# Sharing out the attention loop of a shifted-window block anew: three small VectorE jobs to ScalarE, one to GpSimd, and a new order

## What is computed

```
xn   = layernorm(x) * g1 + b1
xw   = windows(roll(xn, -3, -3))                       # 1024 windows of N=49 tokens
q,k,v = split(xw @ qkv_w + qkv_b)                      # 6 heads of 8
attn = softmax(q * 8**-0.5 @ k.T + rpb + MASK)
out  = (attn @ v) @ proj_w + proj_b
x1   = x + roll(unwindow(out), 3, 3)
h    = layernorm(x1) * g2 + b2
y    = x1 + gelu(h @ fc1_w + fc1_b) @ fc2_w + fc2_b
```

## Time and profile before

| | |
|---|---|
| three runs | 1214.75, 1219.42, 1219.89 us |
| profiled execution | 1203.71 us, its span 1201.9 us |
| busy share of the span | PE 82%, PE weight load 66%, DVE 88%, ACT 77%, POOL 68% |
| mean granted TensorE clock | 0.955 of full speed |
| DMA | 64.50 MB, mean 54 GB/s |
| instructions | 47188 |

### The profile page before, as it was taken

One profiled execution on the slowest core, in us unless ns is written; L12 is line 12 of the kernel. 1 busy time (PEld: TensorE's weight loads), 2 busy tenths in 40 slices (PEclk: granted clock), 3 DMA queues, 4 the chain that ended last, 5 costly groups with the idle time before them and its releaser, 6 DMA issues. The chain is left out here.

```text
span 1201.9 us, 47188 instructions
## 1 busy us (share of the span) xinstructions
PE 990.5 (82%) x16452; PEld 798.1 (66%) x16452; DVE 1055.9 (88%) x2454; ACT 928.1 (77%) x2242; POOL 812.9 (68%) x907
## 2 busy tenths in 40 slices
PE   1588888989888898888888988898882888878877
PEld 0377777777777777777777777777771555555555
DVE  6799899989999999999999999999964888999996
ACT  0378787777877777777787778788773889999997
POOL 6267676666766666666666666677654767888883
PEclk9999999999999999999999999999995889999999
DMA  1122222222222222222222222222210011111111
GB/s 49 38 63 74 63 56 63 67 64 56 60 66 62 61 57 67 65 61 55 60 70 63 56 60 71 64 60 72 54 43 0 29 32 35 35 35 40 35 35 48
DMA packets 87016, 64.50 MB, mean 54 GB/s; under 512 B 53699, under 2 KB 86756, under 8 KB 86966
## 3 DMA queue, kind: packets, MB, share of 16 engines
q1 hardware_dynamic: 86966, 63.83, 20.1%
HBM read 10.48 MB, written 9.63 MB: 17 GB/s over the span
## 5 line engine op out<-in xcount | busy, mean ns | idle before, releaser
L376 POOL TENSOR_TENSOR pl<-p,ph 113x294 f16<-113x294 f32 x512 | 393.2, 777 | 163.8 <-ACT p L435 159.2
L221 POOL TENSOR_TENSOR rstd<-var,mhalf 112x7 f32<-112x7 f32 x128 | 192.6, 1505 | 134.3 <-DVE var L216 134.3
L741 DVE TENSOR_REDUCE rowmax<-banks 113x12 f32<-113x588 f32 x256 | 192.3, 751 | 55.4 <-PE banks L564 52.9
L433 ACT ACTIVATE ph<-banks 113x294 f16<-113x294 f32 x512 | 216.1, 422 | 25.4 <-PE banks L580 21.6
L580 PE MATMUL banks<-Qh,KAg 128*128 128x147 f16 x2048 | 223.7, 232 | 0.0
L435 ACT ACTIVATE p<-banks 113x294 f32<-113x294 f32 x512 | 213.9, 418 | 0.0
L580 PEld LDWEIGHTS banks<-Qh,KAg 128*128 128x128 f16 x2048 | 171.8, 99 | 34.1
L596 PE MATMUL banks<-Vb,ph 113*128 113x36 f16 x3072 | 184.0, 181 | 1.1 <-POOL pl L376 1.1
L596 PE MATMUL banks<-Vb,pl 113*128 113x36 f16 x1536 | 169.4, 180 | 0.0
L596 PEld LDWEIGHTS banks<-Vb,ph 113*128 113x128 f16 x3072 | 161.4, 97 | 11.0 <-POOL pl L376 1.4
L408 ACT ACTIVATE KM<-banks,lorow 128x392 f16<-128x392 f32 x128 | 75.2, 587 | 103.7 <-PE banks L498 103.6
(11 more groups left out here) (120 smaller groups left out, 2891.1 us busy)
## 6 DMA issues: line engine op xcount, KB each, us to landing
Qh<-QAB SPq DMA_DIRECT2D x192, 98.0 KB, 2.2
Vb<-Vn SPq DMA_DIRECT2D x256, 54.0 KB, 2.0
xres<-in_x SPq DMA_DIRECT2D x64, 147.0 KB, 2.2
KAh<-KA SPq DMA_DIRECT2D x192, 49.0 KB, 1.9
out_y<-ybuf SPq DMA_DIRECT2D x64, 147.0 KB, 2.0
Qh<-mT SPq DMA_DIRECT2D x128, 4.6 KB, 2.2
w<-in_weights SPq DMA_DIRECT2D x1, 278.9 KB
mask<-in_maskt SPq DMA_DIRECT2D x1, 257.2 KB
```

Source lines behind the costliest of these rows:

```text
L221: nc.gpsimd.tensor_tensor(rstd[:, :], var[:, :], mhalf[:, :], ALU.pow).then_inc(s_pow, 1)
L376: nc.gpsimd.tensor_tensor(pl[p % 4][:, :, :, 0:N].rearrange("p a w n -> p w a n"), p32[p % 4][:, :, :, :], ph[p % 4][:, :, :, 0:N].rearran ...
L433: nc.scalar.activation(ph[p % 4][:, :, :, 0:N].rearrange("p a w n -> p w a n"), src, ACT.Exp, scale=1.0 / SB)
L741: nc.vector.tensor_reduce(rowmax[:, 2 * p:2 * p + 4, :].rearrange("p (k w) a -> p k (w a)", k=2), sc[0:AP_, :, 0:2 * COLS].rearrange("p k ...
```

## The change

Every instruction of the attention phase is still there, and each computes the same values; four have gone to another engine, and most of the order is new. The MLP phase is not touched.

- `nmean` (the mean of 7 numbers per partition, negated) and `var` go from DVE to ACT, as copies with a scale (and a bias). `var` stands behind the first two exponentials of a step on ACT, `nmean` in the middle of it. Two semaphores that were kept by DVE's order (`s_pow`, `s_xc`) are now waited for by ACT.
- `KAg` of head group 0 goes from DVE to ACT (a copy with the mask column as scale). Group 1 stays on DVE, and moves from the middle of the step to its end. The semaphore `s_kg` becomes two.
- The low part of the output (`otok`, before on DVE line 826) goes to POOL, at the end of its step. DVE's `normalize` of half 0 waits for it.
- PE's transpose of `m16` moves from the end of a step to the start of the next; piece 0 of the plain scores of unit t+1 moves from the start of step t+1 to the end of step t; the `pv`, `t_scores`, `out` and `v` pieces change places.
- On ACT the square moves from the start of a step to the end of the one before, exponential 4 from the end of a step to the start of the next. On POOL the low parts of pieces 3 to 5 move into the next step.

```
+        def ln_mean_scalar(act, n):
+            wait(act, s_xc, n - 1)
+            act.wait_ge(s_sum, n)
+            nc.scalar.activation(nmean[:, :], ssum[:, :], ACT.Copy, scale=-1.0 / C).then_inc(s_mean, 1)
+        def ln_variance_scalar(act, n):
+            act.wait_ge(s_pow, n)
+            act.wait_ge(s_sqsum, n)
+            nc.scalar.activation(var[:, :], sqsum[:, :], ACT.Copy, bias=EPS, scale=1.0 / C).then_inc(s_var, 1)
...
 # GpSimd
+                    low(t - 2, 3)
+                    low(t - 2, 4)
                     ln_rsqrt(pool, t + 3)
+                    low(t - 2, 5)
                     ln_scale(pool, par, t + 3)
...
+                    pool.wait_ge(s_ohi, done(t - 2))
+                    nc.gpsimd.tensor_tensor(otok[:, :, C:2 * C], on[:, :, :], otok[:, :, 0:C],
+                                            ALU.subtract).then_inc(s_olo, 1)
...
 # ScalarE
-                    ln_square(act, par, t + 3)
+                    exp(t - 2, 4)
                     exp(t - 2, 5)
+                    ln_variance_scalar(act, t + 3)
                     k_high(0)
...
                     exp(t - 2, 7)
+                    wait(act, s_st, PAIRS * done(t - 2))
+                    act.wait_ge(s_klow, 2 * done(t))
+                    nc.scalar.activation(KAg[par][:, :, 0, 0:N], KA[par][:, :, :], ACT.Copy,
+                                         scale=grow[:, 0:1]).then_inc(s_kg[0], 1)
                     q_high(0)
+                    ln_mean_scalar(act, t + 4)
...
                     v_high()
-                    exp(t - 1, 4)
+                    ln_square(act, new, t + 4)
...
 # TensorE
+                    pe.wait_ge(s_m16, done(t - 1))
+                        pe.wait_ge(s_vlow, done(t))
+                    nc.tensor.transpose(psT[:, 0:AP_], m16[:, :], idt[0:AP_, 0:AP_]).then_inc(s_mtp, 1)
                     k_piece(0)
-                    scores(t, par, 0)
                     scores(t, par, 1)
-                    pv(t - 2, par, 3)
...
                     t_scores(t - 1, new, 4)
+                    scores(t + 1, new, 0)
                     t_scores(t - 1, new, 5)
+                    pv(t - 1, new, 1)
                     pv(t - 1, new, 2)
-                    pe.wait_ge(s_m16, done(t))
-                        pe.wait_ge(s_vlow, done(t + 1))
-                    nc.tensor.transpose(psT[:, 0:AP_], m16[:, :], idt[0:AP_, 0:AP_]).then_inc(s_mtp, 1)
...
 # VectorE
-                    ln_variance(dve, t + 3)
-                    for g in range(G):
-                        i = block(KAg[par], KA[par][:, :, :], g)
-                    i.then_inc(s_kg, 1)
-                    wait(dve, s_xc, t + 3)
-                    ln_mean(dve, t + 4)
+                    wait(dve, s_olo, done(t - 3))
                     normalize(0)
...
                     v_low()
-                    dve.wait_ge(s_ohi, done(t - 2))
-                    nc.vector.tensor_tensor(otok[:, :, C:2 * C], on[:, :, :], otok[:, :, 0:C],
-                                            ALU.subtract).then_inc(s_olo, 1)
+                    wait(dve, s_st, PAIRS * done(t - 2))
+                    dve.wait_ge(s_klow, 2 * done(t))
+                    block(KAg[par], KA[par][:, :, :], 1).then_inc(s_kg[1], 1)
```

More of the change, by code:

```diff
@@ L156, in swin_block_kernel @@
         s_qg = sem("q_blocks_ready")
-        s_kg = sem("k_blocks_ready")
+        s_kg = [sem(f"k_blocks_of_group{g}_ready") for g in range(G)]
         s_vz = sem("v_blocks_cleared")
@@ L391, in step @@
                 if exists(t - 1):
-                    for p in range(2, 6):
-                        low(t - 1, p)
+                    low(t - 1, 1)
+                    low(t - 1, 2)
+                if exists(t - 2):
+                    pool.wait_ge(s_ohi, done(t - 2))
+                    nc.gpsimd.tensor_tensor(otok[:, :, C:2 * C], on[:, :, :], otok[:, :, 0:C],
+                                            ALU.subtract).then_inc(s_olo, 1)
             def tables():
@@ L459, in step @@
                     ln_high(act, t + 3)
+                if exists(t - 1):
+                    exp(t - 1, 1)
                 if exists(t + 1):
@@ L475, in step @@
                     nc.scalar.activation(otok[:, :, 0:C], on[:, :, :], ACT.Copy).then_inc(s_ohi, 1)
[L476 to L477 removed]
+                if exists(t + 1):
+                    v_high()
+                if exists(t + 3):
+                    ln_square(act, new, t + 4)
             def tables():
@@ L572, in t_scores @@
                         pe.wait_ge(s_tb[upar], blocks_of(u, upar))
-                        pe.wait_ge(s_kg, done(u))
+                        for g in range(G):
+                            pe.wait_ge(s_kg[g], done(u))
                         pe.wait_ge(s_mrow, 16 * G * done(u))
@@ L598, in pv @@
                     i.then_inc(s_pv, 1)
+                if exists(t - 1):
+                    pe.wait_ge(s_m16, done(t - 1))
+                    if exists(t):
+                        pe.wait_ge(s_vlow, done(t))
+                    else:
+                        wait(pe, s_OT, done(t - 4))
+                    nc.tensor.transpose(psT[:, 0:AP_], m16[:, :], idt[0:AP_, 0:AP_]).then_inc(s_mtp, 1)
                 if exists(t + 1):
@@ L635, in step @@
                     pv(t - 2, par, 5)
+                if exists(t):
+                    scores(t, par, 6)
                 if exists(t + 1):
@@ L661, in step @@
                     t_scores(t - 1, new, 4)
+                if exists(t + 1):
+                    scores(t + 1, new, 0)
+                if exists(t - 1):
                     t_scores(t - 1, new, 5)
+                    pv(t - 1, new, 1)
                     pv(t - 1, new, 2)
-                if exists(t):
-                    pe.wait_ge(s_m16, done(t))
-                    if exists(t + 1):
-                        pe.wait_ge(s_vlow, done(t + 1))
-                    else:
-                        wait(pe, s_OT, done(t - 3))
-                    nc.tensor.transpose(psT[:, 0:AP_], m16[:, :], idt[0:AP_, 0:AP_]).then_inc(s_mtp, 1)
             def tables():
@@ L711, in k_low @@
                     if j == 0:
-                        wait(dve, s_kg, done(t - 1))
+                        for g in range(G):
+                            wait(dve, s_kg[g], done(t - 1))
                         wait(dve, s_sb, 16 * HP * done(t - 1))
@@ L779, in step @@
                     ln_sum(dve, t + 3, t + 4)
-                if exists(t - 2):
-                    normalize(0)
                 if exists(t + 1):
                     k_low(1)
+                if exists(t - 2):
+                    invert_sums(0)
                 if exists(t):
                     rmax(4)
-                    wait(dve, s_st, PAIRS * done(t - 2))
-                    dve.wait_ge(s_klow, 2 * done(t))
-                    for g in range(G):
-                        i = block(KAg[par], KA[par][:, :, :], g)
-                    i.then_inc(s_kg, 1)
+                if exists(t - 2):
+                    wait(dve, s_olo, done(t - 3))
+                    normalize(0)
                 if exists(t + 1):
```

32 lines of the change are left out of this document (12 added, 20 removed).

## The result

| | before | changed |
|---|---|---|
| median of the runs | 1217.36 us (1214.75 to 1219.89, 4 runs) | 1130.62 us (1129.78 to 1136.63, 4 runs) |
| ratio, 95% interval | 1 | 0.930 (0.926 to 0.934) |
| profiled execution, its span | 1203.71, 1201.9 us | 1130.22, 1128.4 us |

The account below looks back on a forecast made before the run. DVE was taken to bound the attention phase, with PE next; about 60 steps falling from 13.36 to 12.0 us take 82 us from 1203.7, giving 1122, taken as 1125 us, range 1092 to 1180 us.

Parts of the forecast that it names:

- DVE bounds, PE waits for its tail: Attention step: DVE's 12.3 us plus 0.9 us wait fill it; PE stands 1.2 us before the `m16` transpose, for `v_low`.
- The sum of four jobs, 1.7 us off DVE: `nmean` 0.54, `otok` 0.54, `KAg` 0.58, `var` hardly anything: DVE's need per step falls from 12.3 to 10.6 us.
- What it adds elsewhere: Per step, ACT's need rises from 10.4 to 11.4 us (`KAg`, `var`, `nmean`), POOL's from 9.0 to 10.0 (`otok`).
- PE's need: PE's matmuls in an attention step stay the same, 11.3 us, making PE the next bound.
- The walk's new waits: In one new step, PE loses 0.4 us for low K and 0.25 for `QAg`; DVE loses 0.4 for `xtok`.
- The branch: Loop end on PE: 0.1 of the 0.37 us delay was to stay, 0.05 us a step.
- The clock: PE's lower clock after the double gap costs 1.0 us of that step; granted clock was to be 1.00 throughout.
- The offset of 11 to 16 us between runs and profiled execution: Runs of before lie above their profile; if lower-clock steps cause it, it goes, else the median comes near 1135 us.
- the sum of 1122: Whole kernel: 60 steps x (13.36 - 12.0) = 82 us off the profiled 1203.7 us.
- B: New waits on ACT take more of the gain: step 12.5 to 13.0 us, 1152 to 1182 us; chance 0.15.
- C: Lower clock stays with PE as bound, 1.2 us in every second step: 1172 us; chance 0.08.
- D: ACT becomes the bound through `sqsum`, `var`, `KM`, K half: slower, step 13.7 us, 1237 us; chance 0.05.

Follow-up runs that it names:

- duties_kag_late: Kernel before, old order, `nmean` and `KAg` moved to ACT, low `otok` to POOL, variance left on DVE, `KAg` at the end of ACT's step: step 12.34 us, ratio 0.952.
- order_only: Changed kernel with its new order but all four jobs back on DVE: step 12.77 us, ratio 0.973 to the kernel before.
- duties_only: Kernel before with its old order, the four jobs moved to ACT and POOL: step 13.69 us, ratio 1.014.
- var_km_scores0: Changed kernel with ACT's variance behind the first `KM` and plain scores 0 behind transposed scores 5 on PE: step 11.52 us, 1105.08 us, ratio 0.912.

## Why the prediction was right, and where it was not

The time was to be 1125 us, in a range of 1092 to 1180; measured were 1131. The step was to be 12.0 us and is 12.02. The mechanism came as forecast, but the closeness of both numbers is in part luck, as the points show:

- *DVE bounds, PE waits for its tail.* The first half is shown, in either order: with the new order and the jobs back on DVE, DVE is busy 383 of 400 us, and in the old order, once `KAg` on ACT is out of the way, three jobs less on DVE bring the step at full clock from 13.09 to 12.34 us (duties_kag_late). PE's wait before the transpose was a sign of it rather than a cost of its own: order_only has it before `QAg` in place of the transpose, and duties_kag_late keeps 0.92 us of it.
- *The sum of four jobs, 1.7 us off DVE.* Too high: DVE's busy time fell from 12.3 to 11.0 us and not to 10.6. `KAg` and `otok` together measured 0.96 us a step against the 1.12 that I had taken (0.35 and 0.61 against 0.58 and 0.54). `nmean`, taken at 0.54, is the term that failed: its duration in the rows was a wait for POOL, and such a wait does not leave DVE with the instruction. With `nmean` on ACT the low part of `xtok` takes 773 ns in place of 504, beside a `pl`. That DVE has 0.4 us more to do than forecast did not show in the step, as PE bounds.
- *What it adds elsewhere.* `KAg` on ACT took 967 ns (0.94 expected) and in duties_only 0.86 us of ACT's list (0.82 expected, with an overlap that no row gave), `var` 208 and `nmean` 216 (about 0.15), the subtraction on POOL 930 (0.97). The bound of 0.6 for a tiny ACT instruction was far too wide.
- *PE's need.* PE is busy 11.6 us a step where 11.3 were expected, and idle 0.46 where waits and branch were to make 0.7. The two errors cancel, and that is why 12.0 fits so well.
- *The walk's new waits.* All three came: low part of K 0.26 (0.4), `xtok` 0.32 (0.4), `QAg` 0.39 (0.25). Taking the first and the last away one after the other gave 0.25 and 0.30 us a step, so both were on the path.
- *The branch.* Wrong. I left 0.1 us of it in a pair of steps, since PE's sequencer could run ahead; 0.33 us is still there.
- *The clock.* Right in kind: no even step with a lower clock is left. It had no term of its own; it is a quarter of the gain (0.34 of 1.37 us).
- *The offset of 11 to 16 us between runs and profiled execution.* The four runs of the changed kernel stand 0.4 us below to 6.4 above their profiled one. That the offset was due to steps at the lower clock, as the forecast of 1125 took it, is not shown. Some 7 us or more of it may lie in the MLP phase, which was shorter in the profile of before than in any other. The attention phase gained 79 us and not 82, and the MLP phase of the changed kernel's profile was 6.9 us longer: these two make up the distance between the sum of 1122 and the profiled execution of 1130.
- *Rivals.* B and C did not come. D, ACT becoming the bound through the K halves, is not what the changed kernel does, but what the same jobs do in the old order is near it: duties_only is slower than before. I had argued it down by the transpose's wait moving away, and that comes only with the order. Its path was another than mine, over `xtok` and not over the variance.

The Trainium skill's rule that moving work between VectorE and GpSimd might not help (page Perfetto Trace Analysis, section Optimizing Scalar/DVE Operations) did not decide here: undoing the move costs 0.61 us. Its ground, the port shared under a lock, fits the rows that surprised me: `nmean` 157 ns or 700 beside `pl`, `QAg` 428, 559, 667 or 882 on average, centring 748 or, started beside `xtok`, 1014.

Not settled: why the branch costs PE 0.33 us in the changed kernel while long and short steps are nearly alike in order_only (12.81 and 12.72), where DVE bounds, and in var_km_scores0 (11.53 and 11.51), where PE is busy 99%; and how much of the gain comes from each single move of the order, which was only tried as a whole. Nor was duties_kag_late tried with `otok` or `KAg` alone, so that its 1.10 us has no shares.

## What to carry to other kernels

Before giving work to a less busy engine, follow the rings of waits once round that the new engine's list is part of (here transpose, K half, `KM`, `xtok`, `v_low`), also those that have slack now: once the first bound is relieved, the next ring bounds, and work put into its stretch on the new engine is paid there. The same four moves were worth -0.25 us a step in the old order and +0.70 in the new one; in the old order, three of them with `KAg` 17 instructions further down were worth +1.10. So try the cheap change of place first, before a new order. A tiny VectorE instruction with a long duration may be waiting for GpSimd: see what runs beside it, and ask whether its neighbour will wait in its place once it has moved.

## What the hardware showed that I had not expected

- A loop body of four or of ten steps made PE stop at the branch for up to 4.8 us. With a body of two a long step differs from a short one by 0.33 us in the changed kernel, by 0.46 in the one before, and by 0.1 or less in order_only and var_km_scores0. What holds PE there no run here measures.
- Filling 0.4 of the 1.2 us in which PE was idle with 16 matmuls that nothing reads made the kernel before faster by 2.2%: its steps at full clock stayed as they were (13.09 and 13.10 us), and those at the lower clock went.
- A VectorE instruction of seven elements took 157 ns or 700, the same kind of copy of 784 elements from 414 to 1355 ns (both `QAg` in duties_only). In the rows that were looked at, the long ones have a GpSimd instruction beside them, and the short ones of `nmean` and of `QAg` in duties_only have none.
